# Loading expert results by a count of filled tiles, in a kernel of cross attention and a routed feed-forward layer

## The chip, the cores and the metric

The kernel runs on one core of a Trainium2 chip. The metric is the time of one execution on the device in microseconds (us), the median of several runs. Beside it stands a profile, one execution recorded by the hardware profiler, with a span of its own.

## The reference

Two layers, on `x` of 4 x 1024 tokens of width 256 and a context of 4 x 77 rows:

```python
x = x + align(ctx, layernorm(x))      # a warping path (DTW) per batch: each token gets the sum of the
                                      # context rows that the cheapest path pairs it with
h = layernorm(x)
weights, idx = gate(h)                # softmax over 16 experts in 4 groups; best 2 groups, then best 2 experts
y = sum over the 2 experts of weight * (silu(h @ We1[e] + be1[e]) * (h @ We3[e] + be3[e])) @ We2[e] + be2[e]
z = silu(h @ ws1 + bs1) * (h @ ws3 + bs3) @ ws2 + bs2      # the shared expert, for every token
return x + y + z
```

All data are float32. An expert has 256 x 128, 256 x 128 and 128 x 256 weights; the shared one is twice as wide inside. 4096 tokens with two experts each make 8192 token rows for the experts. How many an expert gets depends on the data.

## The kernel before

The instruction streams of the five engines are written by hand, with semaphores. Only what stands after the alignment matters here.

**Routing and scatter.** The 32 token tiles of 128 tokens are normalised, gated and ranked in groups of eight. GpSimd scatters each row twice into `slot_rows` in the chip's main memory (line 553, 64 indirect DMAs), where every expert has an area of its own. An expert's rows are read back in tiles of 128; the last tile of each is filled up with empty rows. The number of tiles isn't known when the kernel is built, so it always works on `SLOT_TILES` = 79, the most that there can be; those past the filled ones are empty altogether. VectorE works out where each tile lies (`rowtab`, lines 1379 to 1402) from `te`, the tiles of each expert, and `tend`, their running sum.

**The shared expert** takes the tokens in eight chunks of 512. For chunk g, TensorE makes the hidden products in two halves (`shared_h`, line 902, eight matmuls each, line 913), ScalarE takes the silu of a half (line 685), VectorE multiplies the other factor in (`shared_act_half`, line 1240), TensorE makes the output (`shared_z`, lines 927 and 929), and VectorE adds it to `xk`, the running output (`shared_add`, line 1254, two instructions). `EARLY` = 5 chunks are done ahead of the experts, chunks 0 to 2 between the routing groups and chunks 3 and 4 beside the end of the scatters; chunks 5 to 7 come after the experts. TensorE enters the expert pipeline only when `z_used` says that VectorE has added the early chunks (line 1014).

**The expert pipeline** goes over the 79 tiles. SyncE loads a tile's rows into `xs` (line 444), with the row number from a register (line 442) and four buffers; TensorE transposes (line 989), ScalarE copies to `xsT` and, with VectorE, the expert's weights to `w_now` (lines 721 and 1426), TensorE multiplies (line 999), ScalarE and VectorE make `hgT` (lines 730 and 1438), TensorE multiplies again (line 1009), VectorE adds the bias into `ys` (line 1419, the last step of a tile), and GpSimd scatters the rows of `ys` to `results` by token (line 560, eight buffers `ys`, each with a semaphore `res_out[u]`). Rows that stand for nobody have an index out of bounds and aren't written.

**The tail.** SyncE, once through its row loads, waits until all scatters of every buffer u have landed, and then loads the results, 1 MB for four token tiles, into four buffers that lie over the expert weights `w13`:

```python
for u in range(8):
    sp.wait_ge(res_out[u], 16 * len(range(u, SLOT_TILES, 8)))
...
for g in range(4):
    load_results(g)
for g in range(8):
    sp.wait_ge(combined, g + 1)
    if g + 4 < 8:
        load_results(g + 4)
    sp.dma_start(out_nat[...], xk[...])
```

VectorE combines: `combine(g)` multiplies each of the two results of four token tiles by its weight and adds it to `xk` (line 1451, eight instructions), in an order written out at the end among the shared steps. SyncE writes the output of group g after it (line 475). In the tail TensorE goes h(5,0), h(5,1), h(6,0), z(5), h(6,1), h(7,0), z(6), h(7,1), z(7).

Of the kernel before, what the change touches and what calls it, by code (L numbers as in the profile page):

```python
# [3 lines left out]
ALU = mybir.AluOpType  # L4
ACT = mybir.ActivationFunctionType
AX = mybir.AxisListType
F32 = mybir.dt.float32
BF16 = mybir.dt.bfloat16
I32 = mybir.dt.int32

P = 128
# [13 lines left out]
E = 16  # L25
# [14 lines left out]
GT = 8  # L40
EARLY = 5
CONSTS = 9


def build(nc, x, ctx, gate_w, gate_b, we1, be1, we2, be2, we3, be3, ws1, bs1, ws2, bs2, ws3, bs3, out):
# [6 lines left out]
    def sem(name):  # L52
        return nc.alloc_semaphore(name)
# [17 lines left out]
    def place(name, shape, dt=F32, at=None):  # L71

        cursor = top if at is None else at
        off = cursor[0]
        cursor[0] = off + size(shape, dt)
        assert cursor[0] <= nc.sbuf_usable_end, (name, cursor[0])
        return nc.alloc_sbuf_tensor_at(name, shape, dt, offset=off)
# [30 lines left out]
    etab = place("etab", [P, SLOT_TILES], I32)  # L108
    first_row = place("first_row", [P, E])
    fill_row = place("fill_row", [P, E], I32)  # L110
    idx = place("idx", [P, 8], I32)
# [73 lines left out]
    prev_at = cursor[0]  # L185
    prevb = place("prevb", [P, TILES // GT + 1, E], BF16, at=cursor)
    x2T = place("x2T", [P, TOK // 512, KC, 512], at=cursor)
    silu = place("silu", [P, 2, MS, 512], at=cursor)
# [6 lines left out]
    assert cursor[0] <= prev_at  # L195
    back = place("back", [P, 4, 4, 2, D], at=[w13_at])

# [113 lines left out]
    fill_rows_ready = sem("fill_rows_ready")  # L311
    ids_staged = sem("ids_staged")
    tables_ready = sem("tables_ready")
    minus_ready = sem("minus_ready")
# [31 lines left out]
    shared_small = sem("shared_small")  # L346
    tail_in = [sem(f"tail_in{i}") for i in range(4)]
    scattered = [sem(f"scattered{w}") for w in range(2)]
# [13 lines left out]
    with nc.Block() as block:  # L362

        @block.sync
        def _(sp):
# [95 lines left out]
            for u in range(SLOT_TILES % 4):  # L461
                load_later(SLOT_TILES // 4, u)

            for u in range(8):
                sp.wait_ge(res_out[u], 16 * len(range(u, SLOT_TILES, 8)))
            def load_results(g):
                sp.dma_start(back[:, g % 4, :, :, :], results_in[:, 4 * g:4 * g + 4, :, :]).then_inc(tail_in[g % 4], 16)

            for g in range(4):
                load_results(g)  # L470
            for g in range(8):
                sp.wait_ge(combined, g + 1)
                if g + 4 < 8:
                    load_results(g + 4)
                sp.dma_start(out_nat[:, 4 * g:4 * g + 4, :], xk[:, 4 * g:4 * g + 4, 0:D]).then_inc(out_done, 16)
            sp.wait_ge(out_done, 16 * 8)

        @block.gpsimd
        def _(pool):
# [17 lines left out]
            pool.iota(rev_e[:, :], [[-1, E]], base=E, channel_multiplier=0,  # L497
                      allow_small_or_imprecise_dtypes=True).then_inc(const_ready, 1)
            pool.iota(first_row[:, :], [[RG, E]], base=0, channel_multiplier=0,
                      allow_small_or_imprecise_dtypes=True).then_inc(const_ready, 1)  # L500
            for n, (lo, each) in enumerate(((0, TOK // (P // 2)), (P // 2, P // (P // 2)))):
                pool.wait_ge(const_ready, 6 + n)
                pool.iota(base_e[lo:lo + P // 2, :], [[each, E]], base=0, channel_multiplier=0,
                          allow_small_or_imprecise_dtypes=True).then_inc(const_ready, 1)
            pool.wait_ge(const_ready, 8)
            pool.iota(ids[:, :], [[2, TILES]], base=0, channel_multiplier=2 * TILES,
# [518 lines left out]
        def _(dve):  # L1025
# [375 lines left out]
            link(dve.tensor_tensor(rowf[:, :], rowf[:, :], tile_row[:, :], ALU.add))  # L1401
            dve.tensor_copy(rowtab[:, :], rowf[:, :]).then_inc(etab_ready, 1)
            for g in range(TILES // GT, EARLY):
                shared_act_half(g, 0)
                shared_add(g - 1)
                shared_act_half(g, 1)
# [38 lines left out]
            def combine(g):  # L1445

                dve.wait_ge(tail_in[g % 4], 16 * (g // 4 + 1))
                dve.wait_ge(z_used, 2 * g + 2)
                for w in range(2):
                    for T in range(4 * g, 4 * g + 4):  # L1450
                        ins = dve.scalar_tensor_tensor(out=xk[:, T, 0:D], in0=back[:, g % 4, T % 4, w, :],  # L1451
                                                       scalar=wt[:, w, T:T + 1], in1=xk[:, T, 0:D],
                                                       op0=ALU.mult, op1=ALU.add)
                    if w == 0:
                        link(ins)
                ins.then_inc(combined, 1)

            shared_act(5)
            combine(0)
            combine(1)  # L1460
            shared_act_half(6, 0)
            shared_add(5)
            combine(2)
            shared_act_half(6, 1)
            combine(3)
            shared_act_half(7, 0)
            combine(4)
            shared_add(6)
            shared_act_half(7, 1)
            combine(5)  # L1470
            combine(6)
# [22 lines left out]
```

## Time and profile before

| | before |
|---|---|
| median of 3 runs | 499.8 us |
| lowest and highest | 499.48 and 500.84 us |
| the profiled execution | 500.17 us |
| its span | 497.4 us |
| TensorE matmul busy | 346.9 us (70%) |
| VectorE busy | 374.8 us (75%) |
| ScalarE busy | 167.4 us (34%) |
| GpSimd busy | 154.0 us (31%) |
| bytes moved by the DMA queues | 69.07 MB |

Busy time is the time in which an engine executes; waiting, register loads and branches aren't in it. In the profile PE is TensorE, DVE VectorE, ACT ScalarE, POOL GpSimd and SP SyncE; SPq is SyncE's queue, on which DMAs are issued. L444 is line 444 of the kernel. A row of a timeline has the start in us, the time that the row covers, the engine, line and operation, output and inputs, the count, and in brackets how long the engine had idled before and what released it. One execution goes through the alignment (to about 180 us), routing and scatter (to 310), the expert pipeline (312 to 453) and the tail.

### The profile page before, as it was taken

The page shows a single profiled execution, that of the slowest core. Times are in us where ns is not written, and L with a number is a line of the kernel's source. Part 1 is how long each engine was busy: PE and PEld are TensorE (multiplying, and loading weights), DVE is VectorE, ACT ScalarE, POOL GpSimd, SP SyncE. Part 2 cuts the span into 40 slices and gives each one's busy share as a digit, 9 for nine tenths or more (in the row PEclk, how much of TensorE's full clock was granted, in tenths as well). Part 3 has the DMA queues.
Part 4 walks back from the last instruction along what each step waited for, and adds up shares of the span by engine and source line. Part 5 has one row for each costly group of instructions (what it writes and reads, how often), then busy time and mean ns, then how long its engine had stood idle before and what let it go on. Part 6 is the DMA issues. An engine that isn't in the chain of part 4 may idle for free.

```text
span 497.4 us, 10680 instructions
## 1 busy us (share of the span) xinstructions
PE 346.9 (70%) x2315; PEld 261.6 (53%) x2316; DVE 374.8 (75%) x2096; ACT 167.4 (34%) x403; POOL 154.0 (31%) x180
## 2 busy tenths in 40 slices
PE   5850100009994387657968993899899999998981
PEld 4740100009993153333635552788788888884551
DVE  4958999999999649785977832366677777762997
ACT  3654000002212013262626110465556665661110
POOL 8000100000000000366666535155555656553000
PEclk9985555555555575559797998799999999999997
DMA  8404897980001100022222592355445545552994
GB/s 330 184 5 113 260 307 158 235 272 1 26 1 52 48 2 1 32 86 90 92 84 84 186 274 97 81 160 157 129 142 151 155 117 152 138 141 104 384 386 140
DMA packets 48342, 69.07 MB, mean 139 GB/s; under 512 B 10470, under 2 KB 38572, under 8 KB 46639
## 3 DMA queue, kind: packets, MB, share of 16 engines
q1 hardware_dynamic: 41407, 51.76, 35.0%
q0 software_dynamic: 6864, 16.86, 9.5%
q8 instruction: 14, 0.23, 0.2%
q14 instruction: 25, 0.20, 0.1%
q10 hardware_dynamic: 32, 0.02, 0.0%
HBM read 39.33 MB, written 31.24 MB: 142 GB/s over the span
## 4 chain that ended last, share of the span: by engine, by line
DVE 40%; PE 38%; DMA 6%; ACT 6%; issue 5%; POOL 2%; DVEq 1%; SPq 1%; ACTq 0%; POOLq 0%
PE psT L999 14%; PE psT L1009 6%; PE psT L913 5%; DVE xk L1451 5%; DVE V L1201 4%; DVE R L1169 3%; PE psD L989 3%; PE psD L884 3%; DVE A L1207 3%; DVE M L1175 3%; DMA slot_rows<-stage,slot 3%; DMA xs<-slot_rows 2%; POOL slot_rows L553 2%; DVE F L1167 2%; DVE mask L1197 2%
## 5 line engine op out<-in xcount | busy, mean ns | idle before, releaser
L560 POOL DMA_INDIRECT results<-ys,idx x79 | 77.8, 985 | 68.9 <-DVE ys L1419 35.1
L999 PE MATMUL psT<-xsT,w_now 128*128 128x128 f32 x632 | 88.7, 284 | 1.4 <-DVE w_now L1426 0.9
L553 POOL DMA_INDIRECT slot_rows<-stage,slot x64 | 62.4, 975 | 64.9 <-DVE slot L1338 25.9
L999 PEld LDWEIGHTS psT<-xsT,w_now 128*128 128x128 f32 x632 | 78.2, 195 | 6.9 <-issue 3.8
L913 PE MATMUL psT<-x2T,sw 128*128 128x512 f32 x128 | 59.0, 612 | 0.6 <-DVE ys L1419 0.6
L823 PE MATMUL psT<-ident,xk 128*128 128x128 f32 x64 | 15.3, 424 | 60.4 <-DMA xk<-in_x 60.4
L1009 PE MATMUL psT<-w,hgT 128*128 x158 | 48.4, 388 | 0.7 <-DVE hgT L1438 0.7
L721 ACT ACTIVATE w_now<-w 128x256 f32 x79 | 32.9, 417 | 45.7 <-PE psD L989 45.5
L1438 DVE SCALAR_TENSOR_TENSOR hgT<-psT,w,sg 128x128 f32<-128x128 f32 x79 | 27.7, 351 | 27.1 <-ACT sg L730 24.9
L823 PEld LDWEIGHTS psT<-ident,xk 128*128 128x128 f32 x64 | 13.8, 241 | 60.4 <-issue 60.4
L540 POOL IOTA tile_no<- 128x79 f32 x1 | 0.2, 216 | 126.7 <-PE psT L862 126.7
L913 PEld LDWEIGHTS psT<-x2T,sw 128*128 128x128 f32 x128 | 24.6, 197 | 27.8 <-issue 26.6
L989 PE MATMUL psD<-ident,xs 128*128 128x128 f32 x158 | 31.8, 284 | 9.7 <-DMA xs<-slot_rows 9.5
L638 ACT ACTIVATE xT<-psT 128x512 f32<-128x512 f32 x16 | 8.7, 594 | 86.3 <-PE psT L823 86.3
L730 ACT ACTIVATE sg<-psT,w 128x128 f32<-128x128 f32 x79 | 29.0, 367 | 21.8 <-PE psT L999 21.3
L1426 DVE COPY w_now<-w 128x256 f32 x79 | 23.7, 300 | 16.2 <-issue 9.2
L1419 DVE TENSOR_TENSOR ys<-psT,b 128x256 f32<-128x256 f32 x79 | 33.5, 424 | 3.1 <-issue 2.3
L989 PEld LDWEIGHTS psD<-ident,xs 128*128 128x128 f32 x158 | 20.6, 143 | 22.1 <-issue 9.9
L685 ACT ACTIVATE silu<-psT,sb 128x512 f32<-128x512 f32 x16 | 11.0, 688 | 62.3 <-PE psT L913 62.3
L723 ACT ACTIVATE xsT<-psD 128x256 f32<-128x256 f32 x79 | 28.9, 366 | 0.0
L830 PEld LDWEIGHTS psD<-gwT,xT 128*128 128x128 f32 x128 | 28.2, 333 | 0.0
L873 PE MATMUL psC<-ctx_parts,maskT 77*128 77x272 bf16 x96 | 21.4, 380 | 9.6 <-DVE xk L1234 8.6
(223 smaller groups left out, 714.0 us busy)
## 6 DMA issues: line engine op xcount, KB each, us to landing
xs<-slot_rows SPq DMA_DIRECT2D x79, 129.0 KB, 2.3
back<-results SPq DMA_DIRECT2D x8, 1024.0 KB, 7.8
slot_rows<-fill SPq DMA_DIRECT2D x32, 129.0 KB, 4.2
xc<-in_x SPq DMA_DIRECT2D x4, 1024.0 KB, 8.7
xk<-in_x SPq DMA_DIRECT2D x4, 1024.0 KB, 12.1
out<-xk SPq DMA_DIRECT2D x8, 512.0 KB, 7.6
w<-in_L_ffn_We SPq DMA_DIRECT2D x1, 2048.0 KB, 13.1
b<-in_L_ffn_be SPq DMA_DIRECT2D x1, 2048.0 KB, 10.8
```

What stands on the lines that cost most here:

```text
L553: pool.indirect_dma_start(out=slot_rows, out_offset=bass.IndirectOffsetOnAxis(ap=slot[:, w, T:T + 1], axis=0), in_=stage[:, T, :], in_offs ...
L560: pool.indirect_dma_start(out=results, out_offset=bass.IndirectOffsetOnAxis(ap=idx[:, u:u + 1], axis=0), in_=ys[:, u, :], in_offset=None, ...
L721: act.activation(w_now[:, (c + 1) % 2, 1, :], w13f[:, bass.ds(E * WD + e, 2 * I)], ACT.Copy).then_inc(w_act, 1)
L723: act.activation(xsT[:, (c + 1) % 2, :, :].rearrange("p c t -> p (c t)"), psX[(c + 1) % 2], ACT.Copy).then_inc(xT_copied, 1)
L730: act.activation(sg[:, c % 2, :], psH[c % 2][:, 0:P], ACT.Silu, bias=w13f[:, bass.ds(e + D, 1)]).then_inc(silu_done, 1)
L823: mm = pe.transpose(psT[n % 2][c][:, k, :], xk[:, 4 * n + k, c * P:(c + 1) * P], ident[:, :])
L830: mm = pe.matmul(psL[:, 4 * n + k, :], xT[:, n % 2, c, k, :], gwT[:, c, :], start=(c == 0), stop=(c == KC - 1))
L913: mm = pe.matmul(ps_[:, :, :].rearrange("p a b -> p (a b)"), w[:, c, m * P:(m + 1) * P], x2T[:, g, c, :], start=(c == 0), stop=(c == KC - 1))
L989: mm = pe.transpose(psX[r % 2][:, k * P:(k + 1) * P], xs[:, r % 4, k * P:(k + 1) * P], ident[:, :])
L999: mm = pe.matmul(psH[c % 2][:, lo:lo + P], w_now[:, c % 2, k, lo:lo + I], xsT[:, c % 2, k, :], start=(k == 0), stop=(k == KC - 1))
L1009: pe.matmul(psY[(c - 1) % 2], hgT[:, (c - 1) % 2, :], w2f[:, bass.ds(e, D)], start=True, stop=True).then_inc(y_done, 1)
L1419: dve.tensor_tensor(ys[:, r % 8, :], psY[r % 2], b2f[:, bass.ds(e, D)], ALU.add).then_inc(y_read, 1)
```

## The change

- SyncE waits, for each buffer u, for as many scatters as there are filled tiles in it, a number that comes from a register. VectorE computes the eight numbers (`landed`) right after `rowtab`, with three instructions, from the total of filled tiles (the last entry of `tend`) and a constant row `lanes` that GpSimd writes at the start. The wait for all scatters moves to the end of SyncE's stream.
- There are eight result buffers in place of four. Buffers 0 to 3 lie where nothing is in use in the pipeline any more (behind `ys`, over the routing tables, over chunks 4 and 5 of `x2T`) and are loaded once chunk 5's hidden products are done (`h_ready`); buffers 4 to 7 lie over `w13` and are loaded once the last expert product is (`y_done`).
- `EARLY` becomes 6: chunk 5 is done ahead of the pipeline, and two chunks are left for the tail. VectorE's order in the tail now begins with `combine(0)`, with the steps of chunks 6 and 7 between the combinations.

```diff
-EARLY = 5
-CONSTS = 9
+EARLY = 6
+CONSTS = 10
...
+    lanes = place("lanes", [P, 8])
+    landed = place("landed", [P, 8], I32)
...
-    back = place("back", [P, 4, 4, 2, D], at=[w13_at])
+    cursor = [cursor[0]]
+    back = [place(f"back{g}", [P, 4, 2, D], at=cursor) for g in range(2)]
+    assert cursor[0] <= prev_at
+    back += [place("back2", [P, 4, 2, D], at=[low]), place("back3", [P, 4, 2, D], at=[x2T_at + 4 * size([P, KC, 512], F32)])]
+    assert low + size([P, 4, 2, D], F32) <= r_at
+    cursor = [w13_at]
+    back += [place(f"back{g}", [P, 4, 2, D], at=cursor) for g in range(4, 8)]
...
+            sp.wait_ge(landed_ready, 1)
+            sp_landed = [sp.alloc_register(f"sp_landed{u}") for u in range(8)]
             for u in range(8):
-                sp.wait_ge(res_out[u], 16 * len(range(u, SLOT_TILES, 8)))
+                sp.reg_load(sp_landed[u], landed[0:1, u:u + 1])
+            need = [sp.snap(sp_landed[u], min_val=16 * (TOK * 2 // P // 8), max_val=16 * 10) for u in range(8)]
+            for u in range(8):
+                sp.wait_ge(res_out[u], need[u])
+
             def load_results(g):
-                sp.dma_start(back[:, g % 4, :, :, :], results_in[:, 4 * g:4 * g + 4, :, :]).then_inc(tail_in[g % 4], 16)
-
+                sp.dma_start(back[g][:, :, :, :], results_in[:, 4 * g:4 * g + 4, :, :]).then_inc(tail_in[g], 16)
+
+            sp.wait_ge(h_ready, 2 * EARLY)
             for g in range(4):
+                load_results(g)
+            sp.wait_ge(y_done, SLOT_TILES)
+            for g in range(4, 8):
                 load_results(g)
             for g in range(8):
                 sp.wait_ge(combined, g + 1)
-                if g + 4 < 8:
-                    load_results(g + 4)
                 sp.dma_start(out_nat[:, 4 * g:4 * g + 4, :], xk[:, 4 * g:4 * g + 4, 0:D]).then_inc(out_done, 16)
+            for u in range(8):
+                sp.wait_ge(res_out[u], 16 * len(range(u, SLOT_TILES, 8)))
             sp.wait_ge(out_done, 16 * 8)
...
+            pool.iota(lanes[:, :], [[-1, 8]], base=7, channel_multiplier=0,
+                      allow_small_or_imprecise_dtypes=True).then_inc(const_ready, 1)
...
             dve.tensor_copy(rowtab[:, :], rowf[:, :]).then_inc(etab_ready, 1)
+            link(dve.tensor_scalar(te[:, 0:8], lanes[:, :], tend[:, E - 1:E], -3.5, ALU.add, ALU.add))
+            link(dve.tensor_scalar(te[:, 0:8], te[:, 0:8], 0.125, ROUND, ALU.mult, ALU.add))
+            dve.tensor_scalar(landed[:, :], te[:, 0:8], -ROUND, 16.0, ALU.add, ALU.mult).then_inc(landed_ready, 1)
...
-                dve.wait_ge(tail_in[g % 4], 16 * (g // 4 + 1))
+                dve.wait_ge(tail_in[g], 16)
...
-            shared_act(5)
             combine(0)
+            shared_act_half(6, 0)
             combine(1)
-            shared_act_half(6, 0)
-            shared_add(5)
+            shared_act_half(6, 1)
             combine(2)
-            shared_act_half(6, 1)
+            shared_act_half(7, 0)
             combine(3)
-            shared_act_half(7, 0)
-            combine(4)
             shared_add(6)
             shared_act_half(7, 1)
+            combine(4)
             combine(5)
             combine(6)
             shared_add(7)
```

## Rows read from the trace of the kernel before

**Rows 1.** VectorE's timeline in the tail: start, us, engine, line, operation [idle before].

```profile
452.10 0.42 DVE L1419 TENSOR_TENSOR ys<-psT,b 128x256 f32<-128x256 f32 x1 [0.61 <-PE psT L1009]
457.03 0.75 DVE L1240 SCALAR_TENSOR_TENSOR silu<-psT,sb,silu 128x512 f32<-128x512 f32 x1 [4.51 <-ACT silu L685]
460.47 0.75 DVE L1240 SCALAR_TENSOR_TENSOR silu<-psT,sb,silu 128x512 f32<-128x512 f32 x1 [2.68 <-ACT silu L685]
461.13 6.66 DVE L1451 SCALAR_TENSOR_TENSOR xk<-back,wt,xk 128x256 f32<-128x256 f32 x16
...
468.38 1.28 DVE L1254 TENSOR_TENSOR xk<-psC,xk 128x512 f32<-128x512 f32 x2
...
490.65 3.38 DVE L1451 SCALAR_TENSOR_TENSOR xk<-back,wt,xk 128x256 f32<-128x256 f32 x8
```

**Rows 2.** TensorE's timeline in the tail.

```profile
452.57 10.57 PE L913 MATMUL psT<-x2T,sw 128*128 128x512 f32 x24 [0.61 <-DVE ys L1419]
462.98 0.27 PE L927 MATMUL psC<-bs_rows,onesb 96*128 96x256 bf16 x1
...
466.88 7.03 PE L913 MATMUL psT<-x2T,sw 128*128 128x512 f32 x16
```

**Rows 3.** SyncE's queue in time, 444 to 456 us.

```profile
444.29 0.33 SPq L444 DMA_DIRECT2D xs<-slot_rows  x1
455.84 0.33 SPq L467 DMA_DIRECT2D back<-results  x1
```

**Rows 4.** GpSimd's timeline: the scatter of tile 72 and that of tile 78, the last.

```profile
444.08 0.98 POOL L560 DMA_INDIRECT results<-ys,idx  x1 [0.56 <-issue]
...
453.62 0.99 POOL L560 DMA_INDIRECT results<-ys,idx  x1 [0.30 <-issue]
```

**Rows 5.** GpSimd's DMA queue in 443.5 to 445, then 445 to 446.5 us: packets, MB, share.

```profile
q0 software_dynamic: 48, 0.11, 24.9%
...
q0 software_dynamic: 48, 0.01, 3.4%
```

**Rows 6.** VectorE's timeline ahead of the pipeline.

```profile
291.73 0.20 DVE L1402 CAST rowtab<-rowf 128x79 int32<-128x79 f32 x1
292.73 0.75 DVE L1240 SCALAR_TENSOR_TENSOR silu<-psT,sb,silu 128x512 f32<-128x512 f32 x1 [0.80 <-ACT silu L685]
...
304.99 0.69 DVE L1254 TENSOR_TENSOR xk<-psC,xk 128x512 f32<-128x512 f32 x1 [1.26 <-PE psC L929]
```

**Rows 7.** TensorE's timeline from shared chunk 4 into the pipeline.

```profile
300.88 0.28 PE L927 MATMUL psC<-bs_rows,onesb 96*128 96x256 bf16 x1 [1.57 <-DVE silu L1240]
...
312.51 1.43 PE L989 MATMUL psD<-ident,xs 128*128 128x128 f32 x4 [7.56 <-DMA xs<-slot_rows]
314.05 2.08 PE L999 MATMUL psT<-xsT,w_now 128*128 128x128 f32 x8
...
318.72 1.06 PE L999 MATMUL psT<-xsT,w_now 128*128 128x128 f32 x8
...
320.27 1.06 PE L999 MATMUL psT<-xsT,w_now 128*128 128x128 f32 x8
```

**Rows 8.** Stretches: length, each engine's busy us (count), PEclk (granted clock), DMA share, GB/s.

```profile
298.00:302.00 4.00, 2.43 (x11) 1.17 (x10) 0.75 (x1) 0.69 (x1) 2.94 (x4) 1.00 0.42 140
...
314.00:318.00 4.00, 3.95 (x18) 3.96 (x19) 0.77 (x3) 1.75 (x5) 0.00 (x0) 0.50 0.23 60
...
446.00:452.60 6.60, 5.28 (x35) 3.84 (x33) 3.89 (x14) 2.48 (x7) 3.91 (x5) 1.00 0.04 6
...
460.00:464.00 4.00, 4.00 (x14) 2.03 (x13) 3.50 (x8) 1.12 (x2) 0.00 (x0) 1.00 1.01 426
```

**Rows 9.** SyncE's register loads in the pipeline: ns min/median/max, first and last start.

```profile
L442 SPq TENSOR_LOAD <-rowtab x79: 262/308/682, 309.8 to 443.8; - x79
```

**Rows 10.** The page's DMA issues: the results' scatters, median us to landing.

```profile
results<-ys,idx POOLq DMA_INDIRECT x79, 2.9
```

**Rows 11.** The loads of the results, 1 MB each, from issue to landing.

```profile
DMA to landing us min/median/max: 4.5/7.8/10.6
```

More of the change, by code:

```diff
@@ L186, in build @@
     prevb = place("prevb", [P, TILES // GT + 1, E], BF16, at=cursor)
+    x2T_at = cursor[0]
     x2T = place("x2T", [P, TOK // 512, KC, 512], at=cursor)
@@ L312, in build @@
     ids_staged = sem("ids_staged")
+    landed_ready = sem("landed_ready")
     tables_ready = sem("tables_ready")
@@ L346, in build @@
     shared_small = sem("shared_small")
-    tail_in = [sem(f"tail_in{i}") for i in range(4)]
+    tail_in = [sem(f"tail_in{i}") for i in range(8)]
     scattered = [sem(f"scattered{w}") for w in range(2)]
@@ L501, in _ @@
             for n, (lo, each) in enumerate(((0, TOK // (P // 2)), (P // 2, P // (P // 2)))):
-                pool.wait_ge(const_ready, 6 + n)
+                pool.wait_ge(const_ready, 7 + n)
                 pool.iota(base_e[lo:lo + P // 2, :], [[each, E]], base=0, channel_multiplier=0,
                           allow_small_or_imprecise_dtypes=True).then_inc(const_ready, 1)
-            pool.wait_ge(const_ready, 8)
+            pool.wait_ge(const_ready, 9)
             pool.iota(ids[:, :], [[2, TILES]], base=0, channel_multiplier=2 * TILES,
@@ L1450, in combine @@
                     for T in range(4 * g, 4 * g + 4):
-                        ins = dve.scalar_tensor_tensor(out=xk[:, T, 0:D], in0=back[:, g % 4, T % 4, w, :],
+                        ins = dve.scalar_tensor_tensor(out=xk[:, T, 0:D], in0=back[g][:, T % 4, w, :],
                                                        scalar=wt[:, w, T:T + 1], in1=xk[:, T, 0:D],
```

## The prediction

> **What bounds the kernel now.** I read three stretches, each with the view that shows who waits. The tail comes first, on VectorE's timeline [rows 1]. VectorE's last expert addition ends at 452.5 us. It then sits idle for 4.5 us and for 2.7 us, both times waiting for ScalarE's silu of shared chunk 5, and from 461.1 us on it has hardly a gap until the last combination ends at 490.65 + 3.38 = 494.0 us; the last output follows in 3.4 us. So the tail is VectorE's own work plus 7.2 us of idling. TensorE's timeline says why it idles: with nothing left but shared chunks it runs 24 matmuls of chunks 5 and 6 back to back, 3.43 us for every eight [rows 2]. VectorE can't fill the holes, because the results of the experts aren't on chip yet: SyncE issues its last row load at 444.3 us, waits for the scatters, and issues the first load of results at 455.8 us [rows 3]. GpSimd's scatters and the bytes of its queue tell that this wait is mostly for nothing: the scatter issued at 444.08 us is the last with rows (0.11 MB in its window, 0.01 MB in the next), so the six scatters from there to 453.62 us carry only empty slots [rows 4, 5].
>
> The second stretch is ahead of the expert pipeline. TensorE's last shared product is added by VectorE at 304.99 + 0.69 = 305.7 us [rows 6], and TensorE then idles until 312.51 us, 7.56 us, for the load of the first slot rows [rows 7]. Its clock falls meanwhile: 0.50 (1.2 GHz) in 314 to 318 us against 1.00 (2.4 GHz) in 298 to 302 us and in the tail [rows 8]. The third, the pipeline of 79 tiles, is TensorE's, 312.5 to 452.5 us or 1.77 us a tile; the diff changes no instruction in it.
>
> **Chunk 5 moved ahead of the pipeline.** What goes in: a pair of half products (2 x 3.43 us, from eight matmuls each) and the output product of a chunk, 3.9 us from 462.98 to 466.88 us [rows 2]. The schedule there is h(5,0), z(4), h(5,1), z(5): h(5,0) also fills the 1.57 us in which TensorE now waits for VectorE [rows 7], but the same wait comes back before z(5). So VectorE's last addition moves by 3.43 + 3.9 + 3.43 = 10.8 us, from 305.7 to 316.5 us. TensorE may only enter the pipeline then, as it waits for those additions. It started at 312.5 us, so 6.8 of the 10.8 us lie in the old idle time and 4.0 us stick out. GpSimd's scatters and SyncE's row loads don't depend on it.
>
> Part of the 4.0 comes back. Before, the pipeline began on a cold array: from its first transpose at 312.51 us to the product of its third tile at 318.72 us it took 6.2 us, with eight matmuls in 2.08 us instead of 1.06 [rows 7]. In the changed kernel TensorE is busy up to 0.7 us before it, as short a gap as the 1.57 us one, across which the clock stayed at 1.00 [rows 8]. Warm, I build the start from the steady tile: transposes 0.44, copying 0.8, product 0.9, and then two steady tiles of 1.55 us (318.72 to 320.27 us [rows 7]) less a little overlap: about 4.3 us, so the third tile's product starts at 320.8 instead of 318.7 us. I take +2.1 us. The bounds: +4.0 if the start is as cold as before, and +0.5 if the later start also finds slot rows further ahead and loses fewer stalls. VectorE's three small instructions for the counts stand at about 0.28 us each in the 0.80 us that it idles between the table and the next silu product [rows 6]: zero, and if that cover went, 0.8 us on a chain that TensorE doesn't wait for until 3 us later. GpSimd's extra iota takes 0.2 us in the first microseconds, long before its constants are used: zero as well.
>
> **Results loaded early.** SyncE goes through its row loads as before and is free at 444.6 us. Now it loads eight registers. A register load took 0.31 us in the median, 0.26 at least and 0.68 at most [rows 9]; with the range bookkeeping between them eight make about 3.3 us (2.6 to 5.8). It is then at 447.9 us. The scatter of the last filled tile, issued at 444.08 us, lands within the usual 2.9 us [rows 10], at 447.0 us, so it is no longer the wait that comes last. The chunk waits are long met. The first of eight loads of 1 MB took 4.5 us from issue to landing and the fourth 10.6 us when four went together [rows 11], about 2.0 to 2.5 us more for each further MB: buffers 0 to 3 land at 452.4, 454.9, 457.4 and 459.9 us. In 446 to 452.6 us the queues are at 0.04 [rows 8], so little meets them. Buffers 4 to 7 lie over the expert weights and are issued when the last product is done, at about 452 us, behind the first four: landed by 470 us, against use from 472 us. The DMA engines, full at 1.01 in 460 to 464 us [rows 8], run full earlier, and the eight outputs queue behind; all but the last output have the time until 486 us to drain, so I cost this at nothing.
>
> A rule speaks against this part. The trace has 0.31 us for a register load. The Trainium skill, DMA: Bandwidth & Descriptors, section Latency and other measured facts, gives a floor of about 600 ns for a tensor load. By it eight would take 4.8 us and buffer 0 would land at about 454 us, which would cost the tail about 0.5 us; the row, below that floor, decides.
>
> **The new tail**, on the old time scale, E = 452.5 us the end of the last expert addition. One combination is 3.3 us (16 instructions 6.66), a half of a silu product 0.66, the additions of a chunk 1.25 [rows 1]. Combination 0 runs 452.5 to 455.8; the product of chunk 6's first half waits for ScalarE as chunk 5's did, until 457.0, and ends at 457.7; combination 1 to 461.0; second half to 461.6; combination 2 to 464.9; chunk 7's first half to 465.6; combination 3 to 468.9; additions of chunk 6 to 470.1. TensorE in that time: chunk 6 to 459.4, h(7,0) to 462.9, z(6) to 466.8, h(7,1) to 470.2; ScalarE adds 1.0, so the last half product runs 471.2 to 471.9. Then three combinations to 481.8, additions to 483.0 and the last combination to 486.4 us. Against 494.0 us that is 7.6 us less: 2.6 us of VectorE's work have left (2 x 0.66 + 1.25), and of 7.2 us of holes 2.3 are left (455.8 to 457.0 and 470.1 to 471.2). If buffer 0 came by 453.7 us nothing would change, as the first hole has 1.2 us left; later than that each microsecond costs one.
>
> **Sum**, against the profiled execution of 500.2 us (a span of 497.4 and 2.8 around it): 497.4 + 2.1 - 7.6 = 491.9, + 2.8 = 494.7 us. The profiled execution is 0.4 us over the median of the timed runs, 499.8 us, so the median comes to 494.3 us.
>
> **Rivals.**
> A: cold or late. The clock falls in the gap ahead of the pipeline although it is short (+4.0 instead of +2.1), and buffer 0 lands up to 2 us late because register loads run at their longest. For it: 0.68 us loads exist and the array was at half speed at just this point. Against: the gaps of this size kept the clock. 494.3 + 1.9 + up to 1.5: 496.2 to 497.7 us.
> B: the change doesn't load early. If SyncE's wait still ends with the last scatter, buffer 0 is issued at 455.8 and lands at 460.3 us; VectorE's order now puts combination 0 ahead of all shared work, so it idles from 452.5 to 460.3, then combines and multiplies without a hole until 492.0 us: 2.0 us gained, 2.1 lost, 499.9 us. Against: the empty scatters are plain, and the wait counts only full ones.
> C, slower: the pipeline itself gets longer. It takes 1.77 us a tile where 1.55 is its steady step, so 17 us of its 140 are stalls, among them ones in which the sequencers of ScalarE and VectorE load registers late. These depend on how the four engines fall in with one another, and the start, the place of the code and the tables' addresses all move. From 0.07 us a tile (79 x 0.07 = 5.5 us) the gain is gone; at 0.12 us it is 9.5 us and 503.8 us. Against: the loop is the same and three runs lie within 1.4 us. The same mechanism has a lucky side (C'): 0.04 us a tile less, 491.1 us.
> D: the early 4 MB get in the way of what runs at 448 to 452 us, the last tiles and the fetching of code. The Trainium skill, DMA: Bandwidth & Descriptors, section Queues, rings and completion order, says that a DMA engine takes turns between its queues; no row here separates that. From the rows: all row loads are issued before 444.6 us, and in the tail VectorE went on without a gap beside full engines. At most 1 to 2 us, 495.3 to 496.3 us.
>
> **How the numbers follow.** The forecast with its own bounds (492.5 to 496.0 us) gets 0.57, A 0.12, D 0.07, B 0.07, C 0.09, C' 0.08. The range from 491.0 to 498.7 us takes in all but B and C. About 0.3%, 1.5 us, is what a measurement of this kernel can tell from no change: below 498.3 us is faster. Faster 0.57 + 0.12 + 0.07 + 0.08 less 0.02 for the upper ends = 0.82; no change 0.09 (B and those ends); slower 0.09 (C).
>
> **What would show it.** On TensorE's timeline the idle time before the first slot transposes should shrink from 7.56 to under 1 us, with a granted clock of 1.00 at the pipeline's start, and its third product should come some 2 us later. SyncE's first load of results should be issued 4 to 5 us before the last expert addition ends instead of 3.3 us after it. VectorE should start combining within 1 us of its last expert addition and show two holes of about 1.1 us in the tail, which should last 34 instead of 41.5 us. A tile of the pipeline should stay at 1.77 us. The forecast is wrong if the clock is at 0.50 in the first tiles, if buffer 0 lands after 455 us on this scale, or if the pipeline takes over 143 us.

## The result, and the profile after

| | before | changed |
|---|---|---|
| median | 499.96 us (4 runs) | 494.28 us (4 runs) |
| lowest and highest | 499.48 and 500.84 us | 492.81 and 496.60 us |
| ratio of the runs, 95% interval | | 0.9899 [0.9863, 0.9935] |
| the profiled execution, its span | 500.17, 497.4 us | 496.60, 494.8 us |

The change makes the kernel 1.0% faster (ratio 0.9899, its interval ends at 0.9935), and the forecast median was 494.3 us. The profiled execution is the slowest of the four changed runs, 2.3 us over their median, so the sum has to be made against its own span: 2.6 us less than before, not 5.7.

VectorE's timeline in the tail (start, us, engine, line, operation, in brackets the idle time before it and its releaser), to be held against [rows 1]:

```profile
456.94 0.42 DVE L1444 TENSOR_TENSOR ys<-psT,b 128x256 f32<-128x256 f32 x1 [0.62 <-PE psT L1031]
457.34 3.38 DVE L1476 SCALAR_TENSOR_TENSOR xk<-back,wt,xk 128x256 f32<-128x256 f32 x8
461.88 0.75 DVE L1262 SCALAR_TENSOR_TENSOR silu<-psT,sb,silu 128x512 f32<-128x512 f32 x1 [1.16 <-ACT silu L707]
...
476.09 0.75 DVE L1262 SCALAR_TENSOR_TENSOR silu<-psT,sb,silu 128x512 f32<-128x512 f32 x1 [1.06 <-ACT silu L707]
...
488.01 3.38 DVE L1476 SCALAR_TENSOR_TENSOR xk<-back,wt,xk 128x256 f32<-128x256 f32 x8
```

VectorE combines as soon as its last expert addition (line 1444) is done, and the holes of 4.51 and 2.68 us have become 1.16 and 1.06 us. The tail, from the end of that addition at 457.36 to the end of the last combination at 491.39 us, takes 34.0 us instead of 41.5.

What SyncE does for it, from its timeline, its register loads (ns min/median/max), its waits (us in total, times, longest) and the landing of the result loads, against [rows 3], [rows 9] and [rows 11]:

```profile
452.48 6.24 SPq L483 DMA_DIRECT2D back<-results  x8
...
L477 SPq TENSOR_LOAD <-landed x8: 263/267/275, 448.8 to 450.8; - x8
...
SPq L483 <- DMA results<-ys,idx: 0.9, 1, 0.9
...
DMA to landing us min/median/max: 4.8/10.8/16.9
```

The first load goes out 4.9 us ahead of the end of the last expert addition instead of 3.3 us behind it, and takes 4.8 us: buffer 0 lands 0.1 us before it is wanted.

TensorE's timeline where the pipeline starts, against [rows 7]: its first transposes, the first tile's product and the third's.

```profile
316.67 0.41 PE L1011 MATMUL psD<-ident,xs 128*128 128x128 f32 x2 [0.99 <-DVE xk L1276]
...
317.95 1.16 PE L1021 MATMUL psT<-xsT,w_now 128*128 128x128 f32 x8 [0.30 <-ACT xsT L745]
...
321.02 1.06 PE L1021 MATMUL psT<-xsT,w_now 128*128 128x128 f32 x8
```

And the granted clock and DMA share (the last but two and last but one columns) at that place and in the tail, against [rows 8]:

```profile
314.00:318.00 4.00, 2.55 (x14) 1.50 (x12) 1.86 (x5) 0.79 (x3) 0.00 (x0) 1.00 0.13 38
...
456.00:460.00 4.00, 3.28 (x8) 1.54 (x9) 3.35 (x9) 0.00 (x0) 2.83 (x3) 1.00 1.02 424
```

TensorE now waits 0.99 us, for VectorE's addition, where it idled 7.56 us for rows; the clock is at 1.00 (2.4 GHz) instead of 0.50, and the first product takes 1.16 us instead of 2.08.

**Where the time went, in the profiles.** I cut every profile at three moments: the start of the pipeline's first transpose, the start of the third tile's product, and the end of the last expert addition (E). The tail reaches from E to the end of the last combination; the last output adds 3.4 to 3.5 us. In the table the first two columns are times from the start of the span, the others lengths, all in us.

| profile | first transpose | third product | product to E | tail | first result load, from E |
|---|---|---|---|---|---|
| before | 312.5 | 318.7 | 133.8 | 41.5 | +3.3 |
| changed | 316.7 | 321.0 | 136.3 | 34.0 | -4.9 |

So 2.3 us more to the third product, 7.5 less in the tail, and 2.5 us more in the pipeline between, which the sum did not have.

### The profile page after: what moved, and what is told of

Its sections match the earlier page's. It is cut to its first block, busy times and chain, and to the rows that moved or that the text cites. A ratio compares the mean times of both kernels' runs of the same rounds, so it can differ in the third digit from the quotient of the medians.

```text
span 494.8 us, 10697 instructions
## 1 busy us (share of the span) xinstructions
PE 342.3 (69%) x2315; PEld 256.9 (52%) x2316; DVE 375.2 (76%) x2099; ACT 167.1 (34%) x403; POOL 154.3 (31%) x181
## 4 chain that ended last, share of the span: by engine, by line
PE 47%; DVE 37%; ACT 6%; DMA 4%; issue 3%; DVEq 1%; SPq 1%; ACTq 0%
PE psT L1021 13%; PE psT L935 12%; PE psT L1031 5%; DVE V L1223 4%; PE psC L951 4%; DVE R L1191 3%; PE psD L1011 3%; DMA xs<-slot_rows 3%; PE psD L906 3%; DVE M L1197 3%; DVE A L1229 3%; DVE xk L1476 2%; DVE F L1189 2%; DVE mask L1219 2%; DVE M L1187 2%
## 5 line engine op out<-in xcount | busy, mean ns | idle before, releaser
L1021 PE MATMUL psT<-xsT,w_now 128*128 128x128 f32 x632 | 86.6, 280 | 1.9 <-DVE w_now L1451 1.0
L1021 PEld LDWEIGHTS psT<-xsT,w_now 128*128 128x128 f32 x632 | 76.6, 191 | 7.0 <-issue 4.4
L1476 DVE SCALAR_TENSOR_TENSOR xk<-back,wt,xk 128x256 f32<-128x256 f32 x64 | 26.6, 480 | 0.4
```

What stands on the lines that cost most here:

```text
L1021: mm = pe.matmul(psH[c % 2][:, lo:lo + P], w_now[:, c % 2, k, lo:lo + I], xsT[:, c % 2, k, :], start=(k == 0), stop=(k == KC - 1))
L1476: ins = dve.scalar_tensor_tensor(out=xk[:, T, 0:D], in0=back[g][:, T % 4, w, :], scalar=wt[:, w, T:T + 1], in1=xk[:, T, 0:D], op0=ALU.mult ...
```

## The experiments

after_const, loads_only and split5, with their repeats and split5_warm, start from the changed kernel and hold the eight counts, which for these inputs are those of 73 filled tiles, as constants in the waits; the register loads fall away with that. wait_all starts from the changed kernel too, chunk_only and warm_gap from the one before. The matmuls added in three kernels (warm_gap, warm_gap2, split5_warm) write where nothing is read. `...` marks lines left out of a diff. A ratio is to the kernel before, measured on the same chip.

All the profiles, cut as above:

| profile | first transpose | third product | product to E | tail | first result load, from E | ratio to before, 95% interval |
|---|---|---|---|---|---|---|
| before_again | 311.6 | 317.6 | 133.6 | 41.5 | +3.3 | (one run, 497.9 us) |
| loads_only | 313.9 | 319.5 | 133.4 | 38.6 | -5.9 | 0.9908 [0.9875, 0.9940] |
| loads_only2 | 312.9 | 318.4 | 133.7 | 38.6 | -5.8 | 0.9910 [0.9883, 0.9936] |
| chunk_only | 314.8 | 319.2 | 135.8 | 38.9 | +3.3 | 1.0020 [0.9993, 1.0048] |
| wait_all | 316.2 | 320.5 | 133.8 | 41.4 | +3.4 | 1.0063 [1.0035, 1.0091] |
| after_const | 316.4 | 320.8 | 134.7 | 34.0 | -3.8 | 0.9924 [0.9896, 0.9952] |
| after_const2 | 316.6 | 321.0 | 132.7 | 34.0 | -5.6 | 0.9885 [0.9857, 0.9912] |
| after_const3 | 314.6 | 319.0 | 136.5 | 34.0 | -4.8 | 0.9874 [0.9847, 0.9900] |
| warm_gap | 311.1 | 316.8 | 135.3 | 41.5 | +3.3 | 0.9993 [0.9969, 1.0017] |
| warm_gap2 | 314.3 | 318.6 | 135.5 | 41.5 | +3.3 | 0.9976 [0.9953, 0.9999] |
| split5 | 312.5 | 318.5 | 134.6 | 33.8 | -5.6 | 0.9844 [0.9817, 0.9872] |
| split5_warm | 313.9 | 318.3 | 134.9 | 33.8 | -5.6 | 0.9801 [0.9775, 0.9827] |

**after_const: the change, with constants.**

```diff
-                sp.wait_ge(res_out[u], need[u])
+                sp.wait_ge(res_out[u], 16 * len(range(u, 73, 8)))
```

> The changed kernel with the eight counts (for 73 filled tiles) as constants in the waits, so that the eight register loads fall away too and the first load of results can go out 2 to 3 us earlier. My theory: the tail doesn't use this time (buffer 0 landed just at the end of the last expert addition and the first hole behind it has 1.2 us to spare), so as the changed kernel, 494.3 us, tail of 34.0 us from the last expert addition to the end of the last combination. The rival (early loads get in the way of the last tiles): the earlier they go the worse, 1 to 2 us more, and it shows as row loads of the last tiles that land late. Its profile also gives a second measure of the pipeline's length, which was 136.3 us from the third tile's product to the last expert addition in the changed kernel's profile and 133.8 us in that of before: if that is the change's doing it is 136 again, if it is scatter from run to run it may lie anywhere from 133 to 137.

Measured: 494.76 us against 498.64, ratio 0.9924. The tail is 34.0 us in the profile, as in the changed kernel. But the first load of results doesn't go out 2 to 3 us earlier, as I expected: it goes out 3.8 us ahead of E, 1.1 us later than with the register loads (5.6 and 4.8 us ahead in the two repeats). Freed of its register loads, SyncE runs into what comes next, from its waits:

```profile
SPq L485 <- DMA results<-ys,idx: 3.3, 1, 3.3
SPq L480 <- DMA results<-ys,idx: 0.2, 1, 0.2
```

It waits 3.3 us for the scatter of the last filled tile, where it waited 0.9 us with the loads. So the register loads lay wholly beside that scatter and cost nothing. VectorE's timeline shows what the late buffer 0 does:

```profile
456.44 3.43 DVE L1476 SCALAR_TENSOR_TENSOR xk<-back,wt,xk 128x256 f32<-128x256 f32 x8 [1.02 <-DMA back<-results]
```

VectorE waits 1.02 us for it, the hole behind the first combination is gone in exchange, and the tail is as long as before: the slack of 1.2 us that the prediction gave buffer 0 is real. The pipeline took 134.7 us here, between the 133.8 of before and the 136.3 of the changed kernel.

**wait_all: the count taken back.**

```diff
-                sp.wait_ge(res_out[u], need[u])
+                sp.wait_ge(res_out[u], 16 * len(range(u, SLOT_TILES, 8)))
```

> The changed kernel with only the count taken back: SyncE waits for all 79 scatters, with all buffers and the order of the steps as changed. My theory: first load of results 3.3 us after the last expert addition, landed 4.5 us after that; VectorE idles 7.8 us at once, as its order puts a combination first, and then works without a hole; tail 39.5 us instead of 34.0, and 499.9 us in all. The rival, that it is the eight buffers and the chunk and not the count that brings the gain: below 496 us.

Measured: 501.43 us against 498.64, 0.6% slower than before and, by the two ratios, 1.4% slower than after_const on the same chip. VectorE's timeline shows where:

```profile
462.48 3.38 DVE L1476 SCALAR_TENSOR_TENSOR xk<-back,wt,xk 128x256 f32<-128x256 f32 x8 [8.13 <-DMA back<-results]
...
480.46 0.75 DVE L1262 SCALAR_TENSOR_TENSOR silu<-psT,sb,silu 128x512 f32<-128x512 f32 x1 [1.56 <-ACT silu L707]
```

The hole of 8.13 us is the forecast one; the second, 1.56 us, I had missed: each half product stands behind a combination in VectorE's order, TensorE waits for it before the next half (5.04 us ahead of its third eight matmuls of the tail), and so TensorE too ran late to the end. The tail is 41.4 us and not 39.5. What follows: the gain of the change hangs on the count. Without it the new order is worse than the old one: chunk_only, with the same chunk moved and the old order, has a tail of 38.9 us.

**chunk_only: only chunk 5 moved**, in the kernel before.

```diff
-EARLY = 5
+EARLY = 6
...
-            shared_act(5)
+            shared_act(6)
             combine(0)
             combine(1)
-            shared_act_half(6, 0)
-            shared_add(5)
+            shared_act_half(7, 0)
             combine(2)
-            shared_act_half(6, 1)
             combine(3)
-            shared_act_half(7, 0)
+            shared_add(6)
             combine(4)
-            shared_add(6)
```

> Only chunk 5 ahead of the pipeline (EARLY 6), with the four old buffers and the wait for all scatters. My theory: the start of the pipeline costs 2.1 us (third product at 320.8 to 321.1 us), and the tail ends 2.6 us earlier, as VectorE has 2.6 us less work but the same two holes of 4.5 and 2.7 us: 0.5 us faster than before, 499.5 us. If the start were cold (clock at 0.50 in 316 to 322 us), 1.4 us slower, 501.4 us.

Measured: 499.43 us against 498.64, ratio 1.002 with an interval that holds no change and just leaves out the expected 0.999. The tail is 38.9 us, 2.6 less than before as forecast, with the same two holes:

```profile
459.50 0.75 DVE L1240 SCALAR_TENSOR_TENSOR silu<-psT,sb,silu 128x512 f32<-128x512 f32 x1 [4.51 <-ACT silu L685]
462.94 0.75 DVE L1240 SCALAR_TENSOR_TENSOR silu<-psT,sb,silu 128x512 f32<-128x512 f32 x1 [2.68 <-ACT silu L685]
```

The start was warm and the third product came 4.4 us after the first transpose, at 319.2 us instead of the 320.8 to 321.1 that I expected: how early TensorE gets to the pipeline also differs from profile to profile. The tail gave 2.6 us; the third product, 0.5 us later than before, and the pipeline, 135.8 us instead of 133.8, took 2.5. Moving chunk 5 alone brought no gain that can be measured.

**loads_only, loads_only2: only the early loads**, three buffers early and five after the last product, chunk 5 in the tail. The eight buffers and the order that begins with `combine(0)` stay as changed.

```diff
-EARLY = 6
+EARLY = 5
...
             combine(0)
-            shared_act_half(6, 0)
+            shared_act_half(5, 0)
             combine(1)
-            shared_act_half(6, 1)
+            shared_act_half(5, 1)
             combine(2)
-            shared_act_half(7, 0)
+            shared_act_half(6, 0)
+            shared_add(5)
             combine(3)
-            shared_add(6)
-            shared_act_half(7, 1)
+            shared_act_half(6, 1)
             combine(4)
+            shared_act_half(7, 0)
             combine(5)
+            shared_add(6)
+            shared_act_half(7, 1)
             combine(6)
```

> Only the early loads: chunk 5 stays in the tail (EARLY 5), three buffers are loaded early and five after the last expert product, the waits are on constants as in after_const, and the shared steps of chunk 5 stand between the first combinations. My theory: the pipeline starts as in the kernel before (idle of 7.6 us and a cold start ahead of it), and the tail becomes TensorE's: three chunks take it 34 us (2 x 3.43 + 3.9 each, and waits), so VectorE ends 38 us after the last expert addition instead of 41.5: 3.4 us faster than before, 496.6 us. The rival, that VectorE's holes alone count and TensorE is never late: 4.9 us faster, 495.1 us.

> loads_only again, beside after_const3 on one chip, as the first time it came out 0.6 us below after_const where the sum of the parts puts it above. Theory (sum of the measured parts): its tail is 4.6 us longer (38.6 against 34.0) and its third product comes 1.5 to 2.3 us earlier, so 2.3 to 3 us above after_const3. The rival, that chunk 5's move ahead costs about what it brings: within 1 us of after_const3. The length of the pipeline between the two points scatters by 1.5 us from run to run and is no part of either.

Measured: 494.11 us against 498.64 the first time and 495.71 against 500.71 the second, ratios of 0.9908 and 0.9910. The tail is 38.6 us (expected 38), and its late hole is TensorE's, as the timeline of VectorE in loads_only shows:

```profile
457.40 0.75 DVE L1262 SCALAR_TENSOR_TENSOR silu<-psT,sb,silu 128x512 f32<-128x512 f32 x1 [1.23 <-ACT silu L707]
...
482.38 0.75 DVE L1262 SCALAR_TENSOR_TENSOR silu<-psT,sb,silu 128x512 f32<-128x512 f32 x1 [1.58 <-ACT silu L707]
```

By the ratios both gains are about 4.5 us, above my 3.4 (which is still within the intervals) and near the rival's 4.9, though the rival's reason, that TensorE is never late, is not what the trace shows. The tail is 2.9 us shorter than before and the pipeline as long; where the other 1.6 us come from the profiles don't show. The early loads without chunk 5 thus bring most of the whole gain. On its own chip loads_only2 was 1.8 us above after_const3 (495.71 against 493.93), the first time 0.65 us below after_const; the mean of the four ratios of the full change (0.9899, 0.9924, 0.9885, 0.9874) is 0.9896 against 0.9909. The profiles of loads_only and of the three kernels on constants, cut and averaged, put the full change 2.2 us ahead: 4.6 us less tail, against a third product that comes 1.3 us later (320.3 against 319.0 us) and a pipeline that is 1.1 us longer (134.6 against 133.5). So estimates of what chunk 5's move is worth, once the loads are early, run from -0.65 us on one chip to 1.8 on another, with 0.7 by all ratios and 2.2 by the profiles. That it is worth anything isn't shown. My 2.3 to 3 us left the pipeline out, and the rival's "within 1 us" isn't excluded.

**after_const2, after_const3: the same again.**

> after_const again, on the chip of split5 and with more rounds, as 0.8% and 1.0% were measured so far for nearly the same kernel. Theory: 4 to 5 us below before, tail 34.0 us again; a second profile of the pipeline, which shows a stall near the fifth tile if that belongs to the warm, late start, and none if it was chance.

> after_const on the chip of loads_only2 and split5_warm. Theory: 4 to 6 us below before, and 2.3 to 3 us below loads_only2; the rival puts it within 1 us of that kernel. Its pipeline starts warm, 0.99 us after VectorE's wait, in every profile so far.

Measured: 493.78 us against 500.10, and 493.93 against 500.71. The tail is 34.0 us each time. The stretch from the third product to E took 132.7 and 136.5 us: for one and the same kernel, with the 134.7 of the first run, it scatters over 3.8 us. In the chain of work that ended last, the row loads (start, us that the chain spends in one) differ. That of after_const3 has these links:

```profile
322.54 3.99 DMA xs<-slot_rows
335.78 2.93 DMA xs<-slot_rows
349.55 4.01 DMA xs<-slot_rows
446.52 3.82 DMA xs<-slot_rows
```

The median row load takes 2.3 us. In after_const2 the first link of this kind is at 337.70 us, and there is no stall near the fifth tile. So a warm start doesn't always bring that stall. The last one, near 446 us, is in chunk_only too, where no result load goes out before E:

```profile
446.35 3.54 DMA xs<-slot_rows
```

The four profiles with such a link of over 3.5 us past 445 us (changed, chunk_only, after_const3 and warm_gap2) are the four with the longest pipelines, 135.5 to 136.5 us. Late row loads aren't new with the change, though: the chain of before has one too.

```profile
351.62 4.03 DMA xs<-slot_rows
```

**before_again: before, a second profile.**

> The kernel before, unchanged, for a second profile. Theory: third product 6.2 us after the first transpose, no tile of the first ten over 2.3 us, 133 to 134 us from the third product to the last expert addition, tail 41.5 us. If its pipeline takes 135 to 136 us, the 1.5 to 2 us by which the kernels with chunk 5 ahead were longer are chance.

Measured: third product 6.0 us after the first transpose, 133.6 us to E, tail 41.5 us. One tile of the first ten took 2.38 us, against none over 2.3 expected. The pipeline didn't take the 135 to 136 us that would have made the longer ones chance.

**warm_gap, warm_gap2: a warm start alone**, in the kernel before.

```diff
             shared_z(EARLY - 1)
+            warm_up(30)
```

(38 in warm_gap2.)

> The kernel before, with 30 matmuls that nothing uses (bf16, 512 columns, about 0.22 us each) in TensorE's idle time ahead of the pipeline, so that it starts at the same moment but on a warm array. My theory of the prediction: the third tile's product comes 1.9 us earlier and the whole run is 1.9 us shorter. The rival, which the first four runs raised: what the warm start gives is given back, because a fast start runs into the row loads and stalls once more around the fifth tile (2.9 us between two last steps instead of 1.55); then the third product comes 1.9 us earlier but the run is within 0.7 us of before.

> warm_gap with 38 matmuls in place of 30. The first one stopped 1.7 us before the rows arrived and the granted clock fell again (0.83 and 0.74 in 310 to 318 us, first products 1.87 and 1.81 us), so it tested nothing. With 38 the matmuls should reach the moment at which the rows arrive, give or take 1 us by run, and the clock should stay at 1.00. Theory: third product 4.3 us after the first transpose instead of 6.0 to 6.2, and 1 to 2 us below before (less what the matmuls overrun). The rival, that a fast start is given back at the row loads: within 0.7 us of before.

Measured: 499.55 us against 500.10 (0.9993) and 498.92 against 500.71 (0.9976). The first of them stopped too early. TensorE's timeline of warm_gap, then of warm_gap2 in the next fence:

```profile
311.08 0.41 PE L990 MATMUL psD<-ident,xs 128*128 128x128 f32 x2 [1.69 <-DMA xs<-slot_rows]
...
312.37 1.87 PE L1000 MATMUL psT<-xsT,w_now 128*128 128x128 f32 x8
```

```profile
314.25 0.41 PE L990 MATMUL psD<-ident,xs 128*128 128x128 f32 x2 [1.22 <-DMA xs<-slot_rows]
...
315.54 1.16 PE L1000 MATMUL psT<-xsT,w_now 128*128 128x128 f32 x8
...
318.61 1.06 PE L1000 MATMUL psT<-xsT,w_now 128*128 128x128 f32 x8
```

After 1.69 us without work the first product took 1.87 us, after 1.22 us it took 1.16. warm_gap2 did start warm, with 4.4 us to the third product instead of 6.0 to 6.2. It is 1.2 us faster than before (0.0 to 2.4 by the interval), and that interval takes in both theories: it doesn't tell a gain of 1 to 2 us from one below 0.7.

**split5: chunk 5 cut in two**, the halves ahead of the pipeline, the output product and the addition in the tail.

```diff
-            shared_z(EARLY - 1)
...
-            pe.wait_ge(z_used, 2 * EARLY)
+            pe.wait_ge(z_used, 2 * EARLY - 2)
+            pe.wait_ge(act_ready, 2 * EARLY)
...
-            pe.wait_ge(y_read, SLOT_TILES)
             for g in range(EARLY, 8):
                 shared_h(g, 0)
-                if g > EARLY:
-                    shared_z(g - 1)
+                shared_z(g - 1)
+                if g == EARLY:
+                    pe.wait_ge(y_read, SLOT_TILES)
...
-            shared_add(EARLY - 1)
...
             combine(1)
+            shared_add(5)
+            combine(2)
             shared_act_half(6, 1)
-            combine(2)
+            combine(3)
             shared_act_half(7, 0)
-            combine(3)
+            combine(4)
             shared_add(6)
             shared_act_half(7, 1)
-            combine(4)
```

> after_const with chunk 5 split: both of its hidden halves and their silu product ahead of the pipeline, which fill TensorE's idle time up to about 311.8 us and no more, and its output product (3.9 us of TensorE) and addition (1.25 us of VectorE) in the tail, behind the first half of chunk 6, which no longer waits for the last expert addition. Theory: the pipeline starts as early as in the kernel before and warm, the tail is as long as in after_const (about 34 us), so 4 us less than after_const at the start if a warm start keeps its gain, 2 to 3 us less if it gives it back. The rival, that the pipeline's start isn't what chunk 5 costs: no faster than after_const.

Measured: 491.69 us against 500.10, ratio 0.9844, and 2.1 us below after_const2 on the same chip, the lower end of what was expected. The tail is even 0.3 us shorter, though VectorE has 1.25 us more to do in it: the first half of chunk 6 no longer waits for the last expert addition, and the first hole is down to 0.34 us.

```profile
456.75 0.75 DVE L1262 SCALAR_TENSOR_TENSOR silu<-psT,sb,silu 128x512 f32<-128x512 f32 x1 [0.34 <-ACT silu L707]
...
474.87 0.75 DVE L1262 SCALAR_TENSOR_TENSOR silu<-psT,sb,silu 128x512 f32<-128x512 f32 x1 [0.49 <-ACT silu L707]
```

But the start was cold again. TensorE idled 2.98 us for rows:

```profile
312.53 0.41 PE L1010 MATMUL psD<-ident,xs 128*128 128x128 f32 x2 [2.98 <-DMA xs<-slot_rows]
```

**split5_warm: the rest of the gap filled** with 14 matmuls that nothing uses.

```diff
+            for _ in range(14):
+                pe.matmul(psD[1][:, :, :].rearrange("p a b -> p (a b)"), onesb[:, :],
+                          onesb[:, :].unsqueeze(1).to_broadcast([P, 4, P]), start=True, stop=True)
```

> split5 with 14 matmuls that nothing uses behind chunk 5's hidden products, into a bank that is free there, as in split5 TensorE idled 2.98 us ahead of the pipeline and the clock stood at 0.57 in 314 to 318 us, so that its start was as cold as before (5.9 us to the third product). Theory: third product 4.3 us after the first transpose, 1.6 us less than split5, 8 to 10 us below before. The rival (given back): as split5, 7.8 us below before.

Measured: 490.45 us against 500.71, ratio 0.9801 [0.9775, 0.9827], about 10 us below before, and 3.5 us (0.7%) below after_const3 on the same chip, whose interval begins at 0.9847. The same stretch in split5 and split5_warm:

```profile
314.00:318.00 4.00, 4.00 (x21) 4.00 (x22) 0.78 (x3) 1.75 (x5) 0.00 (x0) 0.57 0.25 62
```

```profile
314.00:318.00 4.00, 3.23 (x24) 2.78 (x24) 0.76 (x3) 2.70 (x8) 0.00 (x0) 1.00 0.40 115
```

Clock 1.00 instead of 0.57. By the ratios, 0.9801 against 0.9844, the warm start brings 2.1 us here, though from two chips and with intervals that overlap a little. The two profiles don't show it: the third product comes 4.4 instead of 5.9 us after the first transpose, but the first rows came 1.4 us later in split5_warm, and both tails end at 486.9 us. Together with warm_gap2 the times speak for a gain of 1 to 2 us and against its being given back in full, but they don't prove it. This is the fastest kernel of the study.

## Why the prediction was right, point by point

- **The tail: right in its length and its holes.** 34.0 us was measured where 33.9 was worked out (486.4 less 452.5), holes of 1.16 and 1.06 where 1.2 and 1.1 stood, a first result load at 4.9 us ahead of E where 4.6 stood. The last agrees by two deviations that offset each other: from SyncE's last row load to the first load of results it took 3.8 us and not 3.3, and E came 8.7 us after that row load and not 7.9. loads_only and chunk_only confirm the two halves of it one by one: 38.6 for 38.1 us, 38.9 for 38.9.
- **The register loads: the row was right, and the floor of the Trainium skill was not reached.** Eight loads took 0.27 us each, all within 2.3 us from the first start to the last end, where 3.3 us were forecast. The Trainium skill, DMA: Bandwidth & Descriptors, section Latency and other measured facts, states a floor of about 600 ns for a tensor load; 263 to 275 ns were measured here, so for these loads from on-chip memory the measurement decides. The cost of 0.5 us that the prediction put beside that floor doesn't follow from its own numbers: 444.6 + 4.8 + 4.5 = 453.9 us is 0.2 us past the 453.7 us that buffer 0 had.
- **"It is no longer the wait that comes last": wrong by 0.9 us.** The scatter of the last filled tile was the last to land; SyncE waited 0.9 us for it (3.3 us in after_const). It cost nothing, because buffer 0 was still there 0.1 us ahead of need; in after_const, where it was 1.0 us late, the tail was 34.0 us all the same.
- **The start: right in the mechanism, in its size partly by luck.** Third product at 321.0 for 320.8 us, warm, 4.2 us of TensorE's lateness cut to 2.3. The working names a product of 0.9 us that doesn't belong in it (the third product starts two steps after the first, so 0.44 + 0.8 + 3.1 = 4.3 us); 4.35 us were measured. But with chunk 5 ahead and nothing else different in the stage, the third product came anywhere from 319.0 to 321.0 us, and at 317.6 to 319.5 us in the four profiles that start as before does: on average 1.7 us later, with single profiles 2 us apart. VectorE's three instructions for the counts lay in the idle time as said, with 0.24 of the 0.80 us left:

```profile
291.80 0.22 DVE L1425 TENSOR_SCALAR te<-lanes,tend 128x8 f32<-128x8 f32 x1
292.06 0.17 DVE L1426 TENSOR_SCALAR te<-te 128x8 f32<-128x8 f32 x1
292.26 0.17 DVE L1427 TENSOR_SCALAR landed<-te 128x8 int32<-128x8 f32 x1
292.68 0.75 DVE L1262 SCALAR_TENSOR_TENSOR silu<-psT,sb,silu 128x512 f32<-128x512 f32 x1 [0.24 <-ACT silu L707]
```

- **The pipeline between them: not as steady as I took it.** The sum had no change there. In the profiled execution it was 2.5 us longer, 0.03 us a tile, where rival C would have needed 0.07 to undo the gain. In the four profiles whose kernels start the pipeline as before does, it took 133.4 to 133.8 us; in the ten others 132.7 to 136.5, with a mean of 135.0. The kernels with one of the changed starts thus lose 1.4 us on average, but not each of them: wait_all took 133.8 and after_const2 132.7 us. Single row loads that take 3.5 to 4.4 instead of 2.3 us are where the chain shows the longest. Whether that is brought about by the start or is chance isn't settled: after_const and its two repeats alone cover the whole spread. Why a row load lands late is open too.
- **That the median was hit to the tenth is luck.** The profiled execution had 2.3 (not 2.1) - 7.5 (not 7.6) + 2.5 us for the pipeline (not 0), so a span of about 494.8 instead of 491.9 us. Outside the span came 1.8 instead of 2.8 us, and the median was 2.3 instead of 0.4 us below this execution: 494.3 again. The forecast stood on one profiled execution of before, 0.4 us over its median. On three other chips the medians of before were 498.64, 500.10 and 500.71 us, with single runs from 496.7 to 504.6. The four measurements of the full change, three of them on constants, lie 0.8 to 1.3% below before; the forecast difference was 1.1%.
- **Rival A** didn't happen in the changed kernel, but its mechanism is real: split5 and warm_gap, with 2.98 and 1.69 us of idling, started cold. **Rival B** had the right mechanism and was under-priced: 499.9 us were said, no change; 0.6% (3 us) above before were measured in wait_all. Of these 1.9 us are the tail, 41.4 instead of 39.5 us, because TensorE too runs late in that order; the rest lies within the interval. **Rival C** came about in part in the profiled execution, 0.03 us a tile, and doesn't undo the gain. **Rival D** is refuted for the last row loads: the late ones near 446 to 448 us are issued before any result load and are in chunk_only as well. In loads_only, with results being loaded from 447.0 us on, the last tiles' additions still follow each other every 1.04 to 1.58 us, as in before (1.04 to 1.77).

## What to carry to other kernels

A wait for "all of it" at the end of a pipeline is worth splitting into what is needed and what isn't: counting only the filled tiles, with buffers that are free by then and an order that combines first, let the loads go 8 to 9 us earlier, and this gave 0.9% without moving any shared work. Count, buffers and order weren't told apart further, but without the count the same kernel is slower than before. Ask of every piece of work moved into an idle gap how much of it the gap holds; the part that sticks out can be left behind, as split5 did (another 2.1 us), and a gap that stays can be filled with idle matmuls, which probably gave 1 to 2 us more. And cut two profiles at the same few moments before explaining their difference, since a stretch that nobody touched can differ by more than the effect.

## What the runs showed of the hardware

- Granted clock: idle gaps ahead of the pipeline of 0.99 us (for VectorE) and 1.22 us (warm_gap2) left it at 1.00; after 1.69 us (warm_gap) the first products ran at about half speed, and the clock was at 0.83 in 310 to 314 and 0.74 in 314 to 318 us; after 2.98 us (split5) it was at 0.57. In the kernel before, a gap of 1.57 us inside the shared chunks had left it at 1.00 [rows 7, 8]. So gaps of nearly one length went either way, by what lay around them or by chance.
- The quickest 1 MB load of results landed 4.5 to 5.2 us after its issue in the profiles, the slowest 10.6 to 10.9 us in the kernels with four buffers and 16.9 to 19.0 us in the kernels with eight buffers; with the DMA engines at 1.01 to 1.02 in 456 to 464 us VectorE's combinations kept their 480 ns (474 to 486).
- A load of 129 KB of rows took 2.2 to 2.4 us in the median in the twelve profiles that give it, with single ones up to 4.2 us to landing (split5_warm) and 4.4 us in the chain (the changed kernel at 351.19 us).
